# The first gate of a gated feed-forward stage formed from Tanh instead of Silu

## The reference

```
def _L0_ffn_ref(x, w1_w, w1_s, w2_w, w2_s, h1_w, h1_s, h2_w, h2_s, w3_w, w3_s):
    def _tlin(x, w, s):
        return jnp.einsum('bsi,oi->bso', x, w) * s
    h = jax.nn.silu(_tlin(x, w1_w, w1_s)) * _tlin(x, w2_w, w2_s)
    h = jax.nn.gelu(_tlin(h, h1_w, h1_s), approximate=False)
    h = jax.nn.gelu(_tlin(h, h2_w, h2_s), approximate=False)
    return _tlin(h, w3_w, w3_s)
...
x = x + _L0_ffn_ref(_layernorm(x, axis=-1), ...)
```

## Time and profile before

| | |
|---|---|
| runs, us | 1397.81, 1400.15, 1401.39 |
| median, us | 1400.15 |
| span of the profiled execution, us | 1397.6 |
| that execution's own device time | not given apart; the nearest run is 1397.81 |
| gated stage in the span | about 554 to 919 us |
| PE, DVE, ACT, POOL busy over the span | 85%, 78%, 73%, 47% |

### The profile page before, as it was taken

The page is one execution under the profiler, slowest core; times in us unless marked ns, Lnnn a source line. Parts: engine busy times, 40 slices in busy tenths (PEclk is TensorE's granted clock), DMA queues, the critical chain, the costliest instruction groups (busy, mean ns, idle before and its releaser), DMA issues. The chain is left out here.

```text
span 1397.6 us, 33684 instructions
## 1 busy us (share of the span) xinstructions
PE 1187.9 (85%) x10683; PEld 840.6 (60%) x10683; DVE 1097.0 (78%) x2885; ACT 1015.8 (73%) x2107; POOL 650.3 (47%) x449
## 2 busy tenths in 40 slices
PE   2686767777777775799999999969999999998998
PEld 2454544444444453688888888746666666665886
DVE  3599999999999997567667666437777777777996
ACT  2576566666666664688888888758888888885896
POOL 2766656566565663000000000058888888884110
PEclk8799999999999997899999999989999999999999
DMA  9400000000000000000000000000000000000011
GB/s 243 125 2 1 1 0 0 0 0 0 0 0 0 0 2 2 1 1 0 0 0 0 0 0 0 1 0 2 2 0 0 0 0 0 0 2 2 27 42 53
DMA packets 22080, 17.81 MB, mean 13 GB/s; under 512 B 2369, under 2 KB 17601, under 8 KB 22017
## 3 DMA queue, kind: packets, MB, share of 16 engines
q1 hardware_dynamic: 19792, 16.52, 4.1%
q0 software_dynamic: 352, 0.27, 0.2%
q10 hardware_dynamic: 1872, 0.20, 0.1%
HBM read 12.80 MB, written 4.19 MB: 12 GB/s over the span
## 5 line engine op out<-in xcount | busy, mean ns | idle before, releaser
L647 POOL TENSOR_TENSOR k_heads<-k_t,head_mask 128x2048 f32<-128x2048 f32 x128 | 462.6, 3614 | 57.5 <-ACT k_t L597 57.5
L492 PE MATMUL ps_s<-k_heads,q_t 128*64 128x512 f32 x1024 | 266.4, 640 | 134.7 <-DVE prob L776 133.7
L750 DVE TENSOR_REDUCE top<-ps_s 128x16 f32<-128x1024 f32 x128 | 155.8, 1217 | 111.0 <-PE ps_s L492 110.9
L663 POOL TENSOR_TENSOR rstd<-spread,minus_half 128x1 f32<-128x1 f32 (+2 forms) x140 | 95.0, 678 | 285.1 <-DVE spread L770 198.4
L126 POOL TENSOR_TENSOR front_rstd<-front_spread,minus_half 128x4 f32<-128x4 f32 x32 | 33.4, 1045 | 375.3 <-DVE front_spread L119 375.3
L799 PE MATMUL g_ps<-g_h_lo,w_hi 128*128 128x512 f32 x512 | 206.7, 404 | 0.0
L1015 DVE TENSOR_TENSOR g_h_lo<-g_h,g_h_hi 128x512 fp32r<-128x512 f32 x192 | 132.5, 690 | 92.3 <-ACT g_h_hi L963 88.4
L492 PEld LDWEIGHTS ps_s<-k_heads,q_t 128*64 128x64 f32 x1024 | 74.1, 139 | 217.2 <-issue 208.3
L800 PE MATMUL g_ps<-g_h_hi,w_hi 128*128 128x512 f32 x512 | 202.5, 395 | 0.0
L714 DVE TENSOR_TENSOR y_scale<-rstd,gate 128x1 f32<-128x1 f32 x64 | 171.0, 2671 | 0.1
L591 ACT ACTIVATE prob_t<-ps_pt 128x1024 f32<-128x1024 f32 x128 | 131.0, 1024 | 50.1 <-PE ps_pt L543 50.0
(11 more groups left out here) (171 smaller groups left out, 2503.2 us busy)
## 6 DMA issues: line engine op xcount, KB each, us to landing
out_x<-x_res SPq DMA_DIRECT2D x16, 256.0 KB, 2.3
raw_mid<-in_L_ffn_h_w SPq DMA_DIRECT2D x2, 1024.0 KB, 13.9
x_res<-in_x SPq DMA_DIRECT2D x2, 512.0 KB, 8.0
ctx_res<-in_ctx SPq DMA_DIRECT2D x2, 512.0 KB, 9.3
raw_up<-in_L_ffn_w_w SPq DMA_DIRECT2D x2, 256.0 KB, 7.7
raw_w<-in_L_ffn_W SPq DMA_DIRECT2D x2, 256.0 KB, 5.8
raw_down<-in_L_ffn_w_w SPq DMA_DIRECT2D x1, 256.0 KB, 14.6
raw_l<-in_L_xattn_Wq SPq DMA_DIRECT2D x1, 64.0 KB, 2.1
```

What stands on the lines that cost most here:

```text
L492: last = nc.tensor.matmul(ps_s[b * SEQ:(b + 1) * SEQ, half * 512:(half + 1) * 512], q_t[:, u, b * SEQ:(b + 1) * SEQ], k_heads[:, u % 2, ha ...
L647: nc.gpsimd.tensor_tensor(k_heads[:, s % 2, :, :], k_t[:, s, :].unsqueeze(1).to_broadcast([P, HEADS, P]), t.head_mask[:, :].unsqueeze(2).t ...
L750: nc.vector.tensor_reduce(out=top[:, u % 2, :], in_=ps_s[:, :].rearrange("p (h k) -> p h k", h=HEADS), op=ALU.max, axis=AX.X).then_inc(top ...
```

## The change

`silu` becomes `gated`, with the same two slots. ScalarE writes `tanh(half_s1 * bank)` into it, with `half_s1 = s1 / 2`. VectorE then makes `gated = (gated + 1) * bank` in place, and the product uses `half_s12 = s1 * s2 / 2` as its scale. The new operation has a semaphore, `gated_ready`, on which the product waits. In VectorE's list the new operation of block o comes ahead of the lo of block o-1, and the product of block o behind it. Two small operations form the two new scales ahead of L1058, and ScalarE waits for them.

```diff
-        silu = sb("silu", [P, 2, CHUNK])
+        gated = sb("gated", [P, 2, CHUNK])
+        half_s1 = sb("half_s1", [P, 4])
+        half_s12 = sb("half_s12", [P, 4])
...
-                        nc.scalar.activation(silu[:, o % 2, :], bank(pair(o)), ACT.Silu,
-                                             scale=t.s[:, 0, o:o + 1]).then_inc(silu_ready, 1)
+                        nc.scalar.activation(gated[:, o % 2, :], bank(pair(o)), ACT.Tanh,
+                                             scale=half_s1[:, o:o + 1]).then_inc(tanh_ready, 1)
...
-                wait(act, t.scales_loaded, 16 * 7)
+                wait(act, half_ready, 2)
...
                     for o in range(4):
-                        wait(dve, silu_ready, 4 * i + o + 1)
-
-                        wait(dve, *((lo_ready[0], 4 * i + o - 1) if o > 1 else (lo_ready[1], 4 * i)))
-                        nc.vector.scalar_tensor_tensor(out=h[:, o % 2, :], in0=bank(pair(o) + 1), scalar=t.s[:, 1, o:o + 1],
-                                                       in1=silu[:, o % 2, :], op0=ALU.mult, op1=ALU.mult).then_inc(act_ready[0], 1)
+                        wait(dve, tanh_ready, 4 * i + o + 1)
+                        nc.vector.scalar_tensor_tensor(out=gated[:, o % 2, :], in0=gated[:, o % 2, :], scalar=1.0,
+                                                       in1=bank(pair(o)), op0=ALU.add, op1=ALU.mult).then_inc(gated_ready, 1)
                         if o > 0:
                             split_lo(i, 0, o - 1)
+                        wait(dve, *((lo_ready[0], 4 * i + o - 1) if o > 1 else (lo_ready[1], 4 * i)))
+                        wait(dve, gated_ready, 4 * i + o + 1)
+                        nc.vector.scalar_tensor_tensor(out=h[:, o % 2, :], in0=bank(pair(o) + 1), scalar=half_s12[:, o:o + 1],
+                                                       in1=gated[:, o % 2, :], op0=ALU.mult, op1=ALU.mult).then_inc(act_ready[0], 1)
                     split_lo(i, 0, 3)
...
                 wait(dve, t.scales_loaded, 16 * 7)
+                nc.vector.tensor_scalar(half_s1[:, :], t.s[:, 0, :], 0.5, None, ALU.mult).then_inc(half_ready, 1)
+                dve.wait_ge(half_ready, 1)
+                nc.vector.tensor_tensor(half_s12[:, :], half_s1[:, :], t.s[:, 1, :], ALU.mult).then_inc(half_ready, 1)
+                dve.wait_ge(half_ready, 2)
                 nc.vector.tensor_reduce(out=lo_max[:, :], in_=t.lo_sum[:, :], op=ALU.max, axis=AX.X).then_inc(lo_sum_ready, 1)
```

More of the change, by code:

```diff
@@ L845, in gated_feed_forward @@
         done = [front.up_done, sem("done1"), sem("done2")]
-        silu_ready = sem("silu_ready")
+        half_ready = sem("half_ready")
+        tanh_ready = sem("tanh_ready")
+        gated_ready = sem("gated_ready")
         act_ready = [sem(f"act_ready{n}") for n in range(LEVELS)]
@@ L974, in take_out, with tanh_stage @@
                         nc.scalar.activation(out_t[:, :], ps_out[:, :], ACT.Copy, scale=t.s3[:, 0:1]).then_inc(out_taken, 1)
-                def silu_stage(i, after):
+                def tanh_stage(i, after):
                     if not on(i):
@@ L996, in step @@
                     hidden(j, 1)
-                    silu_stage(j + 1, after=j - 1)
+                    tanh_stage(j + 1, after=j - 1)
                     hidden(j, 2)
-                wait(act, t.scales_loaded, 16 * 7)
+                wait(act, half_ready, 2)
                 steps.run(act, step)
```

## The result

The changed kernel takes 1403.21 us (median of 20 runs, 1398.8 to 1404.51); the kernel before, 1399.71 us in as many. The medians differ by 3.5 us. The ratio is 1.0021, with a 95% interval of 1.0014 to 1.0029: 2.9 us slower, between 2.0 and 4.1, and within the 0.3% that was called no change. The forecast was 1402.4, in a range of 1399.4 to 1406.6.

What follows compares the result with a forecast made beforehand. PE was taken to pace the gated stage, helper work costing only where PE's hand-overs come late. Terms 0.4 + 2.0 + 0.5 - 0.7 = +2.2 us on the median 1400.15 gave 1402.4 us, range 1399.4 to 1406.6.

Steps and rivals of the forecast that it cites:

- The entry: Start of the gated stage: two small VectorE operations ahead of the first reduce delay PE's start, +0.4 us.
- The first product stage: Ahead of step 0: the new operations delay chunk 1's normalise, for which PE idles; PE starts later, +2.0 us.
- Step 0: First step: PE waits less for product 0 but then waits for product 1 at middle(0, 2), +0.5 us.
- The steady steps: Fourteen later steps: PE's turn_back transposes no longer wait for a late take_out; half the gain taken, -0.7 us.
- B: Rival: PE waits for product 1 at middle(j, 2) in every steady step; +5.7 us, 1405.9 us; chance 0.20.
- C: Rival: the table loads stay in the gated stage's steps; +22 us, 1422 us; chance 0.02.
- D: Rival: ACT sets the gated stage's pace after all; 39.8 us off, 1360 us; chance 0.04.

Runs made afterwards that it cites:

- product first: Changed kernel with each block's product directly behind its new operation, ahead of the lo of the block before: 1401.62 us, ratio to before 1.0007.
- loads gone: Kernel before with Tanh in place of Silu and nothing else, so the table loads go and no VectorE work comes: 1397.79 us, ratio 0.9975.
- the operation alone: Changed kernel with Silu in place of Tanh, so the added VectorE operation and the 32 table loads both stay: 1427.83 us, ratio to before 1.0193.
- One more operation: Changed kernel with one more VectorE operation of the same size per block, into a spare tile nothing reads: 1421.61 us, ratio to before 1.0143.

## Why the prediction was right

**The entry, +0.4 forecast:** 0.38 for the two operations by the trace. PE's start lay 0.68 later in this pair; the rest lies within the spread of its branch (4.30 to 4.84 over the profiles).

**The first product stage, +2.0:** 11.89 - 9.93 = 1.96. The forecast took the whole 1.28 of the load as given back; the experiment without the operation shows that only 0.8 of it could be, as PE's slow start holds block 1. In the changed kernel the chain from product 0 to product 1 is long enough to hide all but 0.07 of that wait (the products stand 2.12, 2.05 and 2.05 apart, 2.06 forecast), so there it came back almost whole: with the load kept, A is 1.22 longer. The forecast of 2.0 held because it was made for both parts together.

**Step 0, +0.5:** 13.6 against 13.0 by B corrected, and two more kernels on each side repeat it (13.5 and 13.6 with the changed gate, 13.0 and 13.0 with Silu).

**The steady steps, -0.7:** 21.451 - 21.405 = 0.046, in 13 measured and some 14 steps 0.6 us. Product 1 ended where it was put, 652.54 less the 1.9 us by which the step lies later, against 650.70. The own-semaphore gap was 0.11 (649.63 to 649.74), 0.10 forecast. So the timing was right, but the size of this term is luck. The forecast halved the gain of 0.09 because product 1 might hold PE. It held nothing: the step is as long where product 1 is ready 0.76 us ahead (product first) or 2.16 (loads gone). The transposes gave back the whole 0.09 to 0.10 (0.68 to 0.59 between the matmuls on either side, mean of 13 steps), and some 0.04 of it was lost again in the rest of the step, from `middle(j, 2)` to the next `turn_in` (7.53 to 7.56). Why, no run shows. Two readings in the prediction were off without effect: the silu pairs that it cites stand 21.48 apart and not 21.45, which is right as the mean (21.451), and DVE's new work was put at 2.9 us per step, where 30.8 us in 13.4 steps are 2.3, as neighbouring operations overlap by 0.09.

**The sum:** 0.4 + 2.0 + 0.6 - 0.6 = +2.4, forecast +2.2, and 2.9 (2.0 to 4.1) by the ratio; with the 0.68 of this pair for the entry it is +2.7. The two spans differ by 4.1 us, 1401.7 to 1397.6; what is beyond the sum lies where the clock differed and behind the stage. PE's slow stretch in step 0 was 3 us shorter in the changed kernel's profile, 1.4 us in its favour; near the end of the stage its clock fell (granted 0.50 from 917.6 to 920.5 us, where the kernel before had 1.00), in the last `down`:

```profile
917.28 0.44 PE L799 MATMUL g_ps_out<-g_h_lo,w_hi 128*128 128x512 f32 x1
917.52 0.63 PE L800 MATMUL g_ps_out<-g_h_hi,w_hi 128*128 128x512 f32 x1
...
919.78 1.12 PE L918 MATMUL g_ps_out<-ident,g_out_t 128*128 128x128 f32 x4 [0.78 <-ACT g_out_t L978]
```

and the same transposes before:

```profile
917.80 0.66 PE L914 MATMUL g_ps_out<-ident,g_out_t 128*128 128x128 f32 x4 [0.78 <-ACT g_out_t L974]
```

Matmuls go from 0.40 to 0.63 there and the four transposes take 1.12, where they took 0.66 before; 1.1 us lost. And behind the stage, where no instruction differs, D is 1.7 longer. That accounts for the spans: 2.7 - 1.4 + 1.1 + 1.7 = 4.1. Over the eleven profiles D lies between 479.1 and 480.9; it is short, 479.1 and 479.2, in the kernel before and in the one with the operation alone, and at least 480.5 in the others, so it doesn't follow the kernels; what it follows isn't shown.

**The rivals.** B, product 1 taking the pace, didn't happen. One more operation and the kept loads each made PE wait for product 1 in the steps, but each with a second wait beside it (for the normalised chunk, and for product 0); together they cost 1.2 and 1.4 us per step. C, the loads staying, didn't happen: Tanh and Gelu alternate here with one load in the stage. The operation alone is what it would have been. It was priced 22 us over the kernel before and measured 27, of which the stretches hold 24: 1.33 x 14 per step (forecast 1.2), 3.2 in A and 1.9 in B. D, ACT pacing, is excluded by the kernel that only lost its loads: 3.5 us of 40.

## What to carry to other kernels

An engine that is busy 100% hides the others' work only up to each hand-over: find the moment at which it asks for a result and the moment at which the result is there, since four operations per step were free here with 0.1 us to spare, and four more cost 1.2 us per step. Trading a stall on one helper engine for work on another is neutral only if the room that the stall leaves lies ahead of that work on the same chain. And in a pipeline whose steady steps are covered, look at its first step, where an order made for the steady state (normalise behind the gate) puts work on the path that could run in idle time.

## What was not expected of the hardware

The same own-semaphore wait on VectorE cost 0.03 us in the first product stage (gate 0 from 563.10 for 0.69, product 0 at 563.82), where the engine had been idle before, and 0.10 to 0.11 in the steps; no run separates the cause. PE's granted clock rose from 0.50 to 1.00 at different times after an idle stretch: the slow part of step 0 lasted between 0 and 4.8 us over eleven profiles, which by itself moves a run by 2.2 us. It doesn't follow the length of the idle stretch: 0 behind 3.29 us and 3.2 behind 3.46, 4.8 behind 4.91 and 1.9 behind 6.48. It makes effects of 1 to 2 us hard to see in medians of a dozen runs, while they stand plainly in the distances between landmarks of one trace.
